# Writing out every batch loop of a six-stage decoder kernel

## What is computed

```python
x = x + _L0_attn_ref(_layernorm(x), W_Q, b_Q, W_K, b_K, W_V, b_V, sinks, v_nulls, W_O, W_O_bias)
x = x + _L0_xattn_ref(_layernorm(x), ctx, ctx, Wq, bq, Wk, bk, Wv, bv, scale)   # linear attention
x = x + _L0_ffn_ref(_layernorm(x), Wq, Wk, Wv, Ws, Wd, Wo)          # attention with expert-mixed values
x = x + _L1_attn_ref(_layernorm(x), context, Wq, Wk, Wv, Wout, bout)
x = x + _L1_xattn_ref(_layernorm(x), ctx, ctx, mask, w_q, w_k, w_v, out_w, out_b)
x = x + _L1_ffn_ref(_layernorm(x), w_in, w_out, w1, w2, wg, we, gb, eb)   # shared and routed experts
```

## Time and profile before

| what | value |
|---|---|
| time, 3 runs | 3123.99, 3128.4 and 3128.46 us; median 3128.4 us |
| the profiled execution | span 3124.2 us; its own device time is not listed apart from its span |
| instructions in the trace | 50399 |
| PE busy | 2720.5 us (87%) |
| DVE / ACT / POOL busy | 1999.9 (64%) / 1747.3 (56%) / 792.9 us (25%) |
| instruction transfers | 91 on queue q8 (1.49 MB), 58 on queue q14 (0.48 MB) |

### The profile page before, as it was taken

The page is one execution under the profiler, slowest core; times in us unless marked ns, Lnnn a source line. Parts: engine busy times, 40 slices in busy tenths (PEclk is TensorE's granted clock), DMA queues, the critical chain, the costliest instruction groups (busy, mean ns, idle before and its releaser), DMA issues. The chain is left out here.

```text
span 3124.2 us, 50399 instructions
## 1 busy us (share of the span) xinstructions
PE 2720.5 (87%) x17384; PEld 2036.1 (65%) x17384; DVE 1999.9 (64%) x4360; ACT 1747.3 (56%) x3237; POOL 792.9 (25%) x887
## 2 busy tenths in 40 slices
PE   6778888888876689999979999999979999949998
PEld 3344444444435556777658888888867777748887
DVE  4788778778865756655646666666666556545444
ACT  3888887878874444444435555555555555542221
POOL 1122212222210134444432111111005566610000
PEclk8789889988878899999999999999989999969999
DMA  3000000000001111111010000000010000020000
GB/s 102 4 4 4 0 3 3 0 3 3 1 1 52 68 46 24 24 29 42 21 34 13 6 6 3 6 1 1 1 66 8 8 5 5 2 95 7 3 7 30
DMA packets 88677, 57.76 MB, mean 18 GB/s; under 512 B 55120, under 2 KB 78544, under 8 KB 88016
## 3 DMA queue, kind: packets, MB, share of 16 engines
q1 hardware_dynamic: 88528, 55.80, 6.0%
HBM read 39.00 MB, written 8.39 MB: 15 GB/s over the span
## 5 line engine op out<-in xcount | busy, mean ns | idle before, releaser
L672 DVE SCALAR_TENSOR_TENSOR a_w<-a_w,a_sinks 128x384 f32<-128x384 f32 x512 | 332.8, 715 | 32.0 <-ACT a_w L507 32.0
L2033 POOL TENSOR_SCALAR x_weights<-x_weights,x_sums 128x256 f32<-128x256 f32 x256 | 231.8, 924 | 275.0 <-DVE x_sums L2092 275.0
L1125 POOL TENSOR_SCALAR f_weights<-f_weights,f_sums 128x256 f32<-128x256 f32 x256 | 232.0, 924 | 272.9 <-DVE f_sums L1355 272.9
L486 ACT ACTIVATE a_e<-psum 128x1024 f32<-128x1024 f32 x192 | 195.4, 1018 | 155.7 <-PE psum L345 114.7
L1283 ACT ACTIVATE f_weights<-psum,f_negmax 128x256 f32<-128x256 f32 x256 | 117.7, 472 | 215.2 <-DVE f_negmax L1349 215.2
L1619 ACT ACTIVATE a_turned_w_hi<-psum 128x512 fp32r<-128x512 f32 x256 | 139.1, 596 | 152.0 <-PE psum L1529 151.9
L687 DVE SCALAR_TENSOR_TENSOR a_w<-a_e,psum 128x512 f32<-128x512 f32 x256 | 162.8, 677 | 92.8 <-ACT a_e L488 88.0
L342 PE MATMUL psum<-a_qT,a_kT_half 32*128 32x512 f32 x512 | 165.8, 727 | 60.4 <-DVE a_w L687 49.3
L488 ACT ACTIVATE a_e<-a_e 128x1024 f32<-128x1024 f32 x192 | 202.9, 1057 | 6.1
L2003 ACT ACTIVATE x_weights<-x_masked_s,x_negmax 128x256 f32<-128x256 f32 x256 | 127.0, 497 | 138.6 <-DVE x_negmax L2084 138.6
L1735 DVE TENSOR_REDUCE a_negmax<-psum 128x1 f32<-128x1024 f32 x128 | 156.7, 1224 | 65.7 <-PE psum L123 61.5
(11 more groups left out here) (361 smaller groups left out, 7725.5 us busy)
## 6 DMA issues: line engine op xcount, KB each, us to landing
f_xnT<-all_xnT_all SPq DMA_DIRECT2D x16, 256.0 KB, 2.3
f_pv_rows<-f_pv SPq DMA_DIRECT2D x8, 512.0 KB, 3.1
f_pv_groups<-f_pv_rows SPq DMA_DIRECT2D x8, 512.0 KB
f_w<-in_f_w SPq DMA_DIRECT2D x2, 2048.0 KB, 10.0
all_x_all<-in_x SPq DMA_DIRECT2D x1, 2048.0 KB, 8.4
a_xnT<-all_xnT_all SPq DMA_DIRECT2D x8, 256.0 KB, 2.3
x_xnT<-all_xnT_all SPq DMA_DIRECT2D x8, 256.0 KB, 2.3
x_ctxT<-in_x_ctxT SPq DMA_DIRECT2D x8, 256.0 KB, 2.7
```

The costliest lines, as they stand in the source:

```text
L486: act.activation(e[:, x, :], psS[x], ACT.Exp).then_inc(exp_done, 1)
L672: ins = dve.scalar_tensor_tensor(part, part, sinks[:, col:col + 1], part, ALU.is_ge, ALU.mult)
L1125: ins = pool.tensor_scalar(w, w, sums[:, k, h, t:t + 1], None, ALU.mult)
L2033: ins = pool.tensor_scalar(w, w, sums[:, k, h, t:t + 1], None, ALU.mult)
```

## The change

All loops on the engines are written out; each `Fori` becomes a `for` of Python. Every batch has its own instructions in the program, with constants in place of registers. The calls to `body` are the same, in the same order, with the same flags.

```diff
 def over_batches(eng, body):
-    body(-1, False, True, False)
-    body(0, True, True, False)
-    with eng.Fori(0, B - 2) as i:
-        body(i + 1, True, True, True)
-    body(B - 1, True, False, True)
-    body(B, False, False, True)
+    for b in range(-1, B + 1):
+        body(b, 0 <= b < B, b + 1 < B, b >= 1)
...
-            with sp.Fori(0, B) as b:
+            for b in range(B):
                 sp.wait_ge(v_done, b)
...
-            with sp.Fori(0, B) as b:
+            for b in range(B):
                 sp.wait_ge(projected, b * 3)
...
-            body(0, True)
-            with sp.Fori(0, B - 2) as i:
-                body(i + 1, True)
-            body(B - 1, False)
+            for b in range(B):
+                body(b, b + 1 < B)
...
-            with sp.Fori(0, B) as b:
+            for b in range(B):
                 sp.wait_ge(low, b * (1 + NHID))
...
-            with pe.Fori(0, B) as b:
+            for b in range(B):
                 pe.wait_ge(x_here, b * 16 + 16)
...
-            with act.Fori(0, B) as b:
+            for b in range(B):
                 act.wait_ge(x_here, b * 16 + 16)
...
-            with dve.Fori(0, B) as b:
+            for b in range(B):
                 dve.wait_ge(high, x_split(b))
```

## The result

| kernel | median | runs | lowest to highest |
|---|---|---|---|
| before | 3128.4 us | 5 | 3120.86 to 3132.95 us |
| changed | 3111.5 us | 5 | 3109.2 to 3114.84 us |

The ratio is 0.995, with a 95% interval from 0.9937 to 0.9964. The kernel became faster by 16.9 us by the medians, 15.6 by the ratio, and by 11 to 20 us by the interval. The forecast was 8.3 us, with a range that ended at 3114.5. The direction was right and the size was half of what came. The profiled execution took 3111.32 us, with a span of 3109.4, against 3124.2 before.

A forecast was written before the change was run, and what follows sets the result against it. Engines wait on each other in a ring, PE nearly fills stage 6, and SP's register chain delays PE in stages 2 and 3. Terms -4.6 - 2.0 - 1.7 = -8.3 us take 3128.4 to 3120.1 us, range 3114.5 to 3127.0.

The forecast's parts named there:

- Stage 6, "0": Stage 6, all engines: register instructions run while engines still work on what is queued ahead, so removing them gains 0.
- a rival on the side of no change: Stage 6: two more low-clock stretches of 1.3 us each eat the gain, leaving -5.7 us, 3122.7; chance 0.12.
- Stage 3, -4.6 us: Stage 3, SP: `mix_blocks` transfers issue 1.5 us earlier per batch, cutting PE's waits in six batches, 4.6 us in total.
- Instructions come late: Written-out stages: PE stands still for 53 added code blocks, up to 61 us, 3181; chance 0.06.
- Stage 2, -2.0 us: Stage 2, SP: `ctxT` and `xnT` issue sooner without register instructions, 0.25 us per batch over eight batches.
- Stage 1, -1.7 us: Stage 1, all engines: register instructions lie in the engines' ring; removal saves 1.0 to 2.4 us, the middle taken.
- the wait for `mix_blocks`: Stage 3 rival: PE waits on DVE's `f_attnT` instead, so 4.6 us stay, leaving -3.7 us, 3124.7; chance 0.18.
- Jumps that cost 25 us: Loop stages: 22 passes back wait 1.15 us each for code, so removal gains another 25 us, 3095; chance 0.02.

The follow-up runs named there:

- sp3: Only SP's loop in stage 3 written out, against the kernel before: 3123.67 us beside 3126.86, ratio 0.9991.
- again_after: The changed kernel, all loops written out, run once more unchanged: 3114.51 us against 3127.81 for the kernel before, ratio 0.996.
- only_s12: Only stages 1 and 2 written out, against the kernel before: 3127.65 us beside 3127.55, ratio 1.0002.
- again_before: The kernel before, nothing written out, run once more unchanged: 3128.14 us beside 3127.55, ratio 0.9998.

## Why the prediction was wrong

**Stage 6, "0": the step that failed, worth about 6 us.** I wrote that "the registers run while the engines before them in the queue still work". They don't all: some lengthened a pause of PE from 0.90 to 1.07 us. In time that alone is next to nothing, 0.05 us a batch, so the 0 was nearly right for what the instructions take. What it left out is that the clock answers to the pause. I also gave the clock to a rival on the side of no change, as something "not in the program's hand". In stage 6 it was: 26 long batches of 42 with loops and a pause of 1.06 us or more, none of 35 in the five profiles with 0.90 to 1.01 us, none of 14 without a pause, at 1.5 us a long batch. The earlier trace rows had the price and the earlier trace rows the place; I did not put the two together. The Trainium skill, "TensorE: Matmul & The Clock Gate", section "A second HAM failure mode: psum-queue depth-cycling", tells of a kernel in which short idle times between groups of matmuls were frequent enough to bring the clock down. Stage 6 agrees in part: its clock fell with only two idle times in a batch of 39 us, of 1.06 and 0.50 us.

**Stage 3, -4.6 us: right in mechanism, half delivered.** By itself the edit gave it (sp3). In the changed kernel SP's issues took some 1.3 us longer in three batches, where code blocks came in, and PE's waits kept 2.5 of 4.6 us. If the blocks are the cause, "Instructions come late" was a rival with the wrong victim: PE does not wait for code, but SP's transfers are late.

**Stage 2, -2.0 us: wrong, about 0.** I took the 0.21 us between two issues as SP's register work. The timeline of SP in the changed kernel, a batch:

```profile
1020.19 0.47 SPq L753 DMA_DIRECT2D x_xnT<-all_xnT_all  x1
1020.70 0.59 SPq L754 DMA_DIRECT2D x_ctxT<-in_x_ctxT  x1
```

`ctxT` starts 0.04 us behind `xnT`'s end, as forecast, but its issue now takes 0.59 us in place of 0.43. From the first start to the second end it is 1.10 us, and was 1.13. So the gap that I counted as saved came back in the second issue; why that one takes longer is not shown. What is left, 0.1 us at the head of each batch, shows in some periods, and the late issue at 1002.2 us took it back: from the first batch's projections to the last's it is 67.8 us in both profiles.

**Stage 1, -1.7 us: there, and taken back.** Two batches of the changed kernel's loop stretch, cut at the same place on ACT:

```profile
374.34:483.34 109.00, 92.75 (x444) 49.68 (x444) 85.75 (x150) 88.94 (x88) 25.50 (x34) 0.87 0.01 3
483.34:592.74 109.40, 92.48 (x444) 48.77 (x444) 85.65 (x150) 89.05 (x88) 25.92 (x34) 0.89 0.01 3
```

One is 0.2 us shorter than before's 109.2, one 0.2 longer; they alternate. The piece of the earlier trace rows takes 43.41 us in three of the written-out batches, as batch 7 had it, and 44.3 to 44.5 in the others. Gains and the clock's stretches, which fall differently now, seem to cancel. The end of stage 1, from batch 7's first score product to stage 2's first projection, gained instead. Windows of it, before and then changed:

```profile
807.26:972.33 165.07, 115.18 (x544) 59.90 (x545) 107.56 (x226) 110.95 (x119) 26.30 (x36) 0.77 0.05 12
```

```profile
812.11:973.91 161.80, 111.41 (x545) 57.50 (x545) 107.35 (x226) 110.42 (x119) 26.39 (x36) 0.82 0.05 12
```

3.3 us less, at a higher mean clock (0.82 against 0.77). It was so in five of six profiles with stage 1 written out and in none of eight with its loops. The sixth is again_after, the very same program, so the program alone does not decide it; and only_s12 has it in its profile and no gain in its runs. The cause stays open.

**The sum.** Stage 6 gives about 6 us by three runs, stages 1 to 3 about 2.5 by one, the whole 12.5 to 15.6 by two. The rest, 4 to 7 us, is not settled: the intervals overlap, and the profiles can't add it up, since stages 4 and 5, which the change leaves alone, account for 8.1 us in the first pair of them and for 1.1 in the second (again_before, again_after). **The rivals:** the wait for `mix_blocks` did not turn into one on DVE; PE's wait for `f_attnT` is 10.8 us in sp3, as before. Instructions late on PE: 51 blocks more (53 were forecast), and no wait of PE for code among its waits in stage 3. Jumps that cost 25 us: no, stages 1 and 2 written out, ten of the 22 passes back, gave at most 2.2 us (only_s12), and a batch of stage 6 at full clock became 0.05 us shorter.

## To carry to other kernels

Where TensorE is dense, look at each pause with the granted clock beside it: a tenth of a microsecond more in a pause cost ten times that here (0.98 to 1.07 us, for 0.9 us a batch on average), and the cheapest cure was to move one instruction of another engine out of the pause, with loops or without. Two instructions on one engine that meet end to end may have something between them; compare with a pair that has nothing. A gap between two transfers' issues is work to save only if the second issue does not grow by the same amount.

## What the runs showed of the hardware that was not expected

- A pause of TensorE of 1.06 to 1.15 us was followed by a stretch at the lower clock in 28 of 49 cases in stage 6, one of 0.90 to 1.01 us in none of 35. In stage 3 PE waits 1.8 to 1.9 us for `f_attnT` in each batch, and the clock fell in some batches and not in others, with loops and without.
- An issue by SP with a constant address was not always cheaper than one with registers: `mix_blocks` 323 ns against 278, `ctxT` 594 against 430. From issue to issue the first became faster all the same (460 to 366 ns); `xnT` and `ctxT` together take 1.10 us, and took 1.13.
- Stages with unchanged code (4 and 5) took 1120.7 to 1130.3 us in 14 profiles, with a mean granted clock of 0.97 to 0.98 in the two shown.
- Code blocks that come in can, it seems, hold up SP's issues by some 1.3 us. The Trainium skill, "Runtime: NRT & Kernel Launch", section "Instruction fetch mechanics", calls the cost of a block boundary mostly hidden. For PE the traces agree, with no wait for code among its waits in stage 3. The late issues of SP beside it, at four places in one profile, are another cost, if they come from the blocks.
